# Scatter tables with rows of 128 floats instead of 65 in a graph layer with attention, on one core

## The reference

```
xn = _layernorm(x, axis=-1)                                   # x: 6250 x 512
x = x + gnn(xn, edges) + mix(xn)                              # graph layer, attention
x = x + ffn(_layernorm(x))                                    # one of 16 experts, chosen by the mean token

# gnn: 106,250 edges, each with 64 attributes and a target node dst
summed = segment_sum(edge_attr, dst, num_segments=6250)
count  = segment_sum(ones, dst, num_segments=6250)
agg    = summed / maximum(count, 1)
h      = relu(concatenate([xn, agg]) @ W1 + b1)               # 576 -> 1024
gnn    = xn + h @ W2 + b2
```

## Time and profile before

| | |
|---|---|
| time, median of 2 runs | 2153.27 us (2152.66 to 2153.89) |
| span of the profiled execution | 2151.4 us |
| TensorE (matmul) busy | 1891.4 us, 88% |
| POOL busy | 1365.3 us, 63% |
| DVE busy | 1228.2 us, 57% |
| ACT busy | 559.5 us, 26% |
| DMA queue of SP, share of the 16 engines | 56.0% |
| DMA queue of POOL, share of the 16 engines | 24.8% |
| mean granted TensorE clock | 0.918 |

### The profile page before, as it was taken

One profiled execution on the slowest core, in us unless ns is written; L12 is line 12 of the kernel. 1 busy time (PEld: TensorE's weight loads), 2 busy tenths in 40 slices (PEclk: granted clock), 3 DMA queues, 4 the chain that ended last, 5 costly groups with the idle time before them and its releaser, 6 DMA issues.

```text
span 2151.4 us, 30962 instructions
## 1 busy us (share of the span) xinstructions
PE 1891.4 (88%) x10775; PEld 1511.5 (70%) x10775; DVE 1228.2 (57%) x3855; ACT 559.5 (26%) x1314; POOL 1365.3 (63%) x912
## 2 busy tenths in 40 slices
PE   2799999999999999788776888888745999999798
PEld 1688888888888888544435777777634888887586
DVE  3644354343444332377755666666536888885575
ACT  1422333222333223111131222222212333333210
POOL 4888888888888888588888888888880111011100
PEclk9999999999999999756587998999867999999899
DMA  8978787887777777899799999999857766653884
GB/s 292 227 156 146 136 156 149 164 153 136 153 157 146 133 136 142 203 212 213 144 297 196 199 214 201 211 197 215 155 90 210 232 213 213 209 198 116 284 297 149
DMA packets 522037, 400.76 MB, mean 186 GB/s; under 512 B 355063, under 2 KB 392199, under 8 KB 521882
## 3 DMA queue, kind: packets, MB, share of 16 engines
q1 hardware_dynamic: 392554, 344.12, 56.0%
q0 software_dynamic: 127216, 54.59, 24.8%
q10 hardware_dynamic: 2112, 0.07, 0.1%
HBM read 244.05 MB, written 154.62 MB: 185 GB/s over the span
## 4 chain that ended last, share of the span: by engine, by line
PE 63%; POOL 14%; issue 8%; DMA 7%; DVE 6%; SPq 1%; ACT 1%; ACTq 0%; POOLq 0%; DVEq 0%
PE pr_out_bank L351 26%; POOL table L298 14%; PE gn_acc L351 12%; PE pr_v_bank L351 6%; PE ex_y_bank L351 6%; PE edge_sum L254 5%; DMA table<-edge_sums,edge_row 2%; DVE nm_wide L1049 2%; DMA done<-qk_T 2%; PE nm_io_bank L849 1%; DVE edge_sel L242 1%; PE pr_turn L455 1%; PE gn_h L1847 1%; PE gn_h L1848 1%; PE gn_turn L1838 1%
## 5 line engine op out<-in xcount | busy, mean ns | idle before, releaser
L298 POOL DMA_INDIRECT table<-edge_sums,edge_row x831 | 1317.5, 1585 | 293.7 <-issue 254.0
L242 DVE SCALAR_TENSOR_TENSOR edge_sel<-edge_dst_all,edge_dst_f,upper 128x128 f32<-128x128 int16 x831 | 317.8, 439 | 95.0 <-PE edge_sum L254 91.6
L351 PE MATMUL pr_out_bank<-pr_norm_xT_hi,pr_w_hi 128*128 128x512 f32 (+1 forms) x832 | 329.6, 396 | 0.0
L351 PE MATMUL pr_out_bank<-pr_norm_xT_lo,pr_w_hi 128*128 128x512 f32 (+1 forms) x832 | 321.0, 386 | 0.0
L351 PE MATMUL pr_out_bank<-pr_norm_xT_hi,pr_w_lo 128*128 128x512 f32 (+1 forms) x832 | 320.9, 386 | 0.0
L254 PEld LDWEIGHTS edge_sum<-edge_attr,edge_sel 128*128 128x128 f32 x1662 | 230.7, 208 | 100.2 <-DVE edge_sel L242 62.1
L254 PE MATMUL edge_sum<-edge_attr,edge_sel 128*128 128x65 f32 x1662 | 241.1, 293 | 59.1 <-DVE edge_sel L242 54.4
L264 ACT ACTIVATE edge_sums<-edge_sum 128x260 f32<-128x260 f32 (+1 forms) x209 | 80.6, 386 | 590.8 <-PE edge_sum L254 496.8
L2090 POOL DMA_DIRECT2D x_rows<-gn_x x49 | 26.8, 546 | 275.8 <-DVE gn_x L2005 236.5
L351 PEld LDWEIGHTS pr_out_bank<-pr_norm_xT_lo,pr_w_hi 128*128 128x128 f32 x832 | 156.5, 188 | 34.8
L351 PEld LDWEIGHTS pr_out_bank<-pr_norm_xT_hi,pr_w_lo 128*128 128x128 f32 x832 | 156.9, 189 | 30.3
(11 more groups left out here) (201 smaller groups left out, 3271.9 us busy)
## 6 DMA issues: line engine op xcount, KB each, us to landing
edge_dst_all<-dst SPq DMA_DIRECT2D x103, 256.0 KB
edge_attr<-in_edge_attr SPq DMA_DIRECT2D x103, 256.0 KB
qk_T<-pr_stage SPq DMA_DIRECT2D x48, 512.0 KB
h_pre_T<-pr_stage SPq DMA_DIRECT2D x48, 512.0 KB
gn_pre<-h_pre_T SPq DMA_DIRECT2D x12, 2048.0 KB, 10.0
done<-qk_T SPq DMA_DIRECT2D x16, 1024.0 KB, 6.1
table<-edge_sums,edge_row POOLq DMA_INDIRECT x831
pr_norm_x<-in_x SPq DMA_DIRECT2D x12, 1024.0 KB
```

The source lines that it names most:

```text
L242: op = dve.scalar_tensor_tensor(out=self.sel[q][0:rows, j, 0:rows], in0=self.dst_all[k][0:rows, t:t + m * (rows - 1) + 1:m], scalar=self.d ...
L298: pool.indirect_dma_start(self.c.table[t], bass.IndirectOffsetOnAxis(ap=self.row[k][0:rows, j:j + 1], axis=0), self.sums[k][0:rows, j, :], ...
L351: mm = pe.matmul(out, a, c, start=first and i == 0, stop=last and i == n - 1)
```

## The change

There are three edits.

1. The tables get rows of `TCOLS` = 128 floats (512 bytes) instead of 65 (260 bytes), and so does the tile `edge_sums` that the scatters read. Each scatter moves all 128 floats of a row. Columns 65 to 127 of `edge_sums` are cleared once at the start, by four more memsets on DVE, on which SP's first load and ACT's first copy now wait. `gnn` loads only the first 65 columns of each row.
2. The zeros: a table is now 3.28 MB instead of 1.66 MB. The tile `zero` has 640 columns instead of 1625, and each partition of it is written ten times instead of twice. In a few words the change was called "zeros written in larger packets"; by the code a run of zeros was 6500 bytes and is now 2560.
3. The larger `edge_sums` takes 8 KB more of each partition. To fit, buffers of `attend` (`near`, `r_hi`, `kt`) are placed in another order, and three small ones (`gate`, `weight`, `total_inv`) are given back before `attend`. No wait is added or removed by that.

```
@@
+TCOLS = 128
+ZROWS = 5
@@ class Edges
-        self.sums = sb("sums", [P, BATCH, ECOLS])
+        self.sums = sb("sums", [P, BATCH, TCOLS])
@@
     def begin_sp(self, sp):
-        sp.wait_ge(self.ones_set, SLOTS)
+        sp.wait_ge(self.ones_set, 2 * SLOTS)
 
     def begin_dve(self, dve):
         for k in range(SLOTS):
             dve.memset(self.attr[k][:, :, EDIM:ECOLS], 1.0).then_inc(self.ones_set, 1)
+            dve.memset(self.sums[k][:, :, ECOLS:TCOLS], 0.0).then_inc(self.ones_set, 1)
         dve.sem_inc(self.summed, 2)
 
     def begin_act(self, act):
+        act.wait_ge(self.ones_set, 2 * SLOTS)
         act.sem_inc(self.kept, 2)
@@
-        act.activation(self.sums[k][0:rows, j0:j0 + w, :], self.p_sum[q][0:rows, 0:w * ECOLS]
+        act.activation(self.sums[k][0:rows, j0:j0 + w, 0:ECOLS], self.p_sum[q][0:rows, 0:w * ECOLS]
@@ project_stage
-        zero = sb("zero", [P, TROWS // P * ECOLS // 2])
+        zero = sb("zero", [P, ZROWS * TCOLS])
@@
     def zero_table(sp, t):
-        sp.dma_start(c.table[t].rearrange("(p b a) c -> p b (a c)", p=P, b=2),
-                     zero[:, :].unsqueeze(1).to_broadcast([P, 2, TROWS // P * ECOLS // 2])
+        parts = TROWS // P // ZROWS
+        sp.dma_start(c.table[t].rearrange("(p b a) c -> p b (a c)", p=P, b=parts),
+                     zero[:, :].unsqueeze(1).to_broadcast([P, parts, ZROWS * TCOLS])
@@
-        sp.wait_ge(edges.ones_set, SLOTS + 1)
+        sp.wait_ge(edges.ones_set, 2 * SLOTS + 1)
@@ attend_stage
-        near = [[sb(f"near{g}_{half}", [P, 4, P]) for half in range(2)] for g in range(2)]
+        near = [[sb(f"near{g}_0", [P, 4, P])] for g in range(2)]
+        r_hi = [sb(f"r_hi{k}", [P, CH, P], F32R) for k in range(2)]
...
-        kt = [sb(f"kt{u}", [P, P, HEADS]) for u in range(2)]
+        kt = [sb("kt0", [P, P, HEADS])]
+        for g in range(2):
+            near[g].append(sb(f"near{g}_1", [P, 4, P]))
+        kt.append(sb("kt1", [P, P, HEADS]))
@@ gnn_stage, load_tables
-                    sp.dma_start(agg_raw[:, t, :, :], c.table[t][bass.ds(b * BT, n), :]
+                    sp.dma_start(agg_raw[:, t, :, :], c.table[t][bass.ds(b * BT, n), 0:ECOLS]
@@ kernel_body
+        c.table = [nc.dram_tensor(f"sums_table{t}", [TROWS, TCOLS], F32, kind="Internal").ap() for t in range(TABLES)]
```

More of the change, by code:

```diff
@@ L1258, in attend_stage @@
         bias_out = rest[0]
-        r_hi = [sb(f"r_hi{k}", [P, CH, P], F32R) for k in range(2)]
         r_lo = [sb(f"r_lo{k}", [P, CH, P], F32R) for k in range(2)]
-        kt = [sb(f"kt{u}", [P, P, HEADS]) for u in range(2)]
+        kt = [sb("kt0", [P, P, HEADS])]
+        for g in range(2):
+            near[g].append(sb(f"near{g}_1", [P, 4, P]))
+        kt.append(sb("kt1", [P, P, HEADS]))
         x.append(sb("x1", [P, CH, DIM]))
@@ L1686, in sb @@
             return ctx.enter_context(nc.sbuf_tensor(what, shape, F32))
-        c.gate, c.weight, c.total_inv = sb("gate", [P, NG, HEADS]), sb("weight", [P, NG, HEADS]), sb("total_inv", [P, HEADS])
         c.mix0 = sb("mix0", [P, BT // GT, P])
@@ L1691, in front_stages @@
         c.mix_sb = c.done[:, 0:NG * HEADS * HEADS].rearrange("p (g f) -> p g f", g=NG)
-        with nc.sbuf_tensor("inverse", [P, NG, 2 * HEADS], F32) as c.inverse, \
+        with nc.sbuf_tensor("gate", [P, NG, HEADS], F32) as c.gate, \
+                nc.sbuf_tensor("weight", [P, NG, HEADS], F32) as c.weight, \
+                nc.sbuf_tensor("total_inv", [P, HEADS], F32) as c.total_inv, \
+                nc.sbuf_tensor("inverse", [P, NG, 2 * HEADS], F32) as c.inverse, \
                 nc.sbuf_tensor("kept", [P, CH * TOKENS], F32) as c.kept:
@@ L1787, in load_tables @@
                 if n == BT:
-                    sp.dma_start(agg_raw[:, t, :, :], c.table[t][bass.ds(b * BT, n), :]
+                    sp.dma_start(agg_raw[:, t, :, :], c.table[t][bass.ds(b * BT, n), 0:ECOLS]
                                  .rearrange("(s p) e -> p s e", p=P)).then_inc(table_in, 16)
                 else:
-                    sp.dma_start(agg_raw[0:n, t, 0, :], c.table[t][bass.ds(b * BT, n), :]
+                    sp.dma_start(agg_raw[0:n, t, 0, :], c.table[t][bass.ds(b * BT, n), 0:ECOLS]
                                  ).then_inc(table_in, 16)
```

## The result

The changed kernel took 2172.84 us (2172.55 to 2173.12, two runs) against 2153.27 us: ratio 1.0088, 95% interval 1.0069 to 1.0107, slower by 19.6 us. The forecast was 2177 us, and the time is in its range. The profiled execution has a span of 2171.4 us, 20.0 us above that of before.

What follows compares the result with a forecast made beforehand. TensorE's path, started late by zeros queued ahead of the tokens, bounds the kernel up to POOL's long wait, then POOL's scatters. 21.5 + 1.9 = 23.4 us on a 2151.4 us span, plus 1.9 for timed runs: 2177 us, range 2140 to 2205.

Steps and rivals of the forecast that it cites:

- The zeros and the memsets: At the start: five larger tables' zeros ahead of the tokens cost +21.5 us, four more memsets +1.9 us.
- The joint: POOL's one long wait, 16.06 us after `project`'s last batch: before it TensorE's path rules, after it POOL sets the end.
- POOL's scatters: POOL's time for each scatter stays 1558 ns, as bytes a row do not count: 0 us.
- A: Rival: POOL's scatters become cheaper, 1558 down to 1024 ns, total 2133 us; chance 0.06.
- D: Rival: POOL's scatter instruction grows by more than 0.05 us, total 2196 us and more; chance 0.04.
- The transfers: Scatter packets in POOL's DMA queue grow 9 to 19 ns in `project` and `attend`; 0 us on the path.
- Rival C: Scatter transfers slow `project` and `attend`, an add's price going with its bytes: about 2335 us; chance 0.13.
- Buffers in another order: In `attend`: the new order of buffers moves no instruction, so it costs 0 us.
- Attention 4 to 8.5% longer by the transfers: In `attend`: larger scatter packets on full DMA engines could lengthen it by 19 to 38 us, covered by waits.
- The cover: Around `attend`: DVE's 19.45 us idle and ACT's 26.5 us for POOL's slots, 46 us, hide its lengthening.

Runs made afterwards that it cites:

- zeros_twice: Kernel before the change, with the zeros of its first five tables sent a second time to unused tables, rows still 65 floats; 2176.23 us, ratio 1.0100.
- weights_at_32: Kernel before the change, with two pads so that the projection weights begin at 32 above a multiple of 512 bytes; 2148.99 us, ratio 0.9979.
- two_tables_later: Kernel before the change, with zeros of tables 3 and 4 moved behind the first tokens and edge batch 2; 2148.11 us, ratio 0.9979.
- both: Kernel before the change, with weights_at_32 and two_tables_later together, rows of 65 floats; 2141.03 us, ratio 0.9940.
- tokens_first_after: Changed kernel, with SP's first transfers reordered so that one table's zeros instead of five stand ahead of the tokens; 2188.10 us, ratio 1.0168.
- rows160: Changed kernel, with rows of 160 floats (640 bytes) scattered whole and zeros in packets of 640 bytes; 2221.11 us, ratio 1.0317.
- attention_order: Kernel before the change, with only the new order and places of the attention buffers, old tables and zeros; 2151.72 us, ratio 0.9994.

## Why the prediction was right

**The zeros and the memsets** (21.5 + 1.9 us) came out at 22.7 together. The packets went at 402 GB/s, faster than the 388 that was taken from packets of 2048 bytes, and the four memsets took 1.91 us. zeros_twice shows that this term goes through to the end undiminished.

**The joint** was read rightly: POOL waits there once, before and after; what happens before it on TensorE's path moves the end, as long as that wait is not used up. zeros_twice (+21), weights_at_32, two_tables_later and both (-4 to -12) are all this one sentence. Its other half, what happens when the wait is gone, no run shows purely: in tokens_first_after 2.80 us of it were left. The joint came at 921 us and the last scatter at 1631, not at 927 and 1639, by the 6 us of the product stage.

**POOL's scatters** (0): 1558 ns at 260 and 512 bytes, 1557 at 256 and 640. Rivals A and D are out.

**The transfers.** POOL's queue in the changed kernel, from 100 to 600 and from 1167 to 1517 us, against the earlier trace rows:

```profile
q0 software_dynamic: 38481, 17.53, 37.7%
q0 software_dynamic: 26547, 12.10, 31.9%
```

By the prediction's own measure, the mean of that queue's packets, one went from 69 to 78 ns in `project` and from 55 to 67 in attention: +9.5 and +12, in the lower half of the 9 to 19. The median scatter packet went from 48 to 65 ns, +17; mean and median differ because a part of the packets takes far longer than the rest. The queue's shares, 37.7% and 31.9%, are in the forecast's 38 to 42 and 30 to 35, or just under. POOL waited for landings 23.1 us in all instead of 15.6, at most 0.3 us at a time in attention. Rival C is out. The Trainium skill ("DMA: Bandwidth & Descriptors", section "Specifications") says that a transfer under 512 bytes is a read, modify and write in the engine, and that only from there on is line rate reached. These packets show no step at 512 bytes: the medians at 256, 260, 512 and 640 bytes lie near one line, and 260 bytes take less time than 512.

**Buffers in another order: 0** was the step that failed. It took "no instruction moves" for "no time moves". Two things moved: the weights' tile and with it the product stage, -6.0 us, which hid a quarter of the zeros' price from the total and is the main reason why the time came out 4 us under the forecast; and attention, where the new layout alone took 8 us or so more than the old order's mean of 465 us, in one profile. That the total came so near is in part luck: -6.0 and -1.6 us stand against +0.7, +2.6 and +1.7, and none of the five was forecast.

**Attention 4 to 8.5% longer by the transfers** gave the right size, 4.8%, for a reason that carries at most a part: with the new order, 256 or 260 bytes gave 473 to 487 us and 512 bytes 474 to 488. That is luck as well. The cover, called nearly used up, was overdrawn by 2.6 us. The prediction had added two waits up to 46 us, but only DVE's 19.45 us lay between attention's end and the tables. ACT's 26.5 us for POOL's slots are gone in the changed kernel, and attention took 22 us more all the same; how much longer it would be without their going, no run shows.

What stays open: what in the buffers' new order and places makes the packets of 1024 bytes dearer. Alignment to 64 bytes and the tables' place in HBM were tried, and neither brings 70 ns back; rows160 has the new order and took 71 ns, so the order is not enough by itself; places at multiples of 256 bytes, as before the change, were not tried in the new order. Open is also how the granted clock of attention and its length hang together, since each can follow from the other. Over the whole of attention the clock was 0.88 before and 0.83 after; at the same mean of 0.84 `both` took 468 us and attention_order 473, in one profile each, so the clock does not account for all of it. And open are the 1.7 us more in `gnn` and `expert`.

## What to carry to other kernels

A change of shape moves every tile that is allocated after it: compare the addresses of the hot matmuls' operands before and after, and try a few hundred bytes of padding before explaining a few us with the change itself. Where two engines' paths meet at one wait, every saving or cost ahead of it on the later path goes through to the end while the other still waits there, so note the length of that wait first; it is a guide and no exact budget, since a change ahead of it can move both paths. A transfer is as late as what stands ahead of it in its queue: two tables' zeros moved behind the tokens gained, while putting the tokens ahead of four tables lost time (ratio 1.0168 against 1.0088 for the change), since the next edge batch behind them came no earlier and the scatters had no table to go to.

## What the runs showed of the hardware

- The time of a product (128 x 128 by 128 x 512, float32r, full clock) went with the places of its two operands in a partition. Taken as the moving operand's place less the loaded one's, modulo 256 bytes, both kinds of bank fall in one row, though the loaded operand is the weights in the output banks and the tokens in the v banks: 227 ns at 0, 229 and 230 at 64, 231 and 232 at 128, 233 at 192. From the worst mix to 0 that is 12 us of 810.
- An indirect scatter that adds costs POOL 1557 to 1558 ns for 128 rows at 256, 260, 512 and 640 bytes a row; only the packets grow, by 0.066 ns a byte at the median.
- Zero packets of 2560 bytes took 102 ns alone, and 102 to 113 beside other transfers in all stretches of 2 us but two. Those of 2600 bytes took 105 ns at first and then up to 200, 180 of them where nothing else ran (26 to 28 us). The runs do not show why.
